# A fused layer stack: the last tiles and the last chunk of each stack issued in an order of their own

## What is computed

```python
x = x + 0.5 * _L0_ffn_ref(_layernorm(x, axis=-1), ...)   # stack 1: six layers
x = x + _L0_attn_ref(_layernorm(x, axis=-1), ...)        # a Mamba block
x = x + 0.5 * _L0_ffn_ref(_layernorm(x, axis=-1), ...)   # stack 2: the same six layers
...
for i in range(DEPTH):                                   # DEPTH = 6
    x = attn_layer(shift_tokens(x), Wqkv[i], q_scale[i], k_scale[i], Wo[i]) + x
    x = ffn_layer(shift_tokens(x), ln_g[i], ln_b[i], W1[i], b1[i], W2[i], b2[i]) + x
```

## Time and profile before

| | us |
|---|---|
| median of three runs | 3400.14 |
| lowest, highest | 3398.57, 3403.94 |
| the profiled execution | 3398.57 |
| its span, from the first to the last instruction | 3396.5 |
| stack 1 up to its last write of X | 1554.9 |
| TensorE busy | 3189.6 (94%) |
| VectorE, ScalarE, GpSimd busy | 2794.0, 2514.8, 2434.8 |

### The profile page before, as it was taken

One profiled execution on the slowest core, in us unless ns is written; L12 is line 12 of the kernel. 1 busy time (PEld: TensorE's weight loads), 2 busy tenths in 40 slices (PEclk: granted clock), 3 DMA queues, 4 the chain that ended last, 5 costly groups with the idle time before them and its releaser, 6 DMA issues.

```text
span 3396.5 us, 120279 instructions
## 1 busy us (share of the span) xinstructions
PE 3189.6 (94%) x51528; PEld 2517.5 (74%) x51528; DVE 2794.0 (82%) x3179; ACT 2514.8 (74%) x3154; POOL 2434.8 (72%) x1225
## 2 busy tenths in 40 slices
PE   7999999999999999986787999999999999999997
PEld 5888887887888888773223788878788888788775
DVE  6888888888888888865997888888888888888884
ACT  5777777777777777766775677777777777777765
POOL 6777776777777777640998777768768768678662
PEclk9999999999999999998999999999999999999999
DMA  3333233333233333221000322323323323333222
GB/s 117 88 76 88 66 88 83 77 77 91 72 83 86 77 77 76 65 64 40 8 1 1 87 72 70 94 66 88 90 70 82 91 64 89 83 77 83 68 63 55
DMA packets 142010, 245.21 MB, mean 72 GB/s; under 512 B 32365, under 2 KB 34350, under 8 KB 141358
## 3 DMA queue, kind: packets, MB, share of 16 engines
q1 hardware_dynamic: 141486, 237.51, 27.5%
HBM read 35.01 MB, written 1.05 MB: 11 GB/s over the span
## 4 chain that ended last, share of the span: by engine, by line
PE 75%; DVE 8%; issue 7%; POOL 5%; ACT 4%; DMA 0%; DVEq 0%; SPq 0%; POOLq 0%; ACTq 0%
PE PS L254 14%; PE PS L380 11%; PE PS L198 8%; PE PS L402 7%; PE PS L200 7%; PE PS L199 7%; PE PS L315 6%; PE PS L507 4%; ACT ARENA L740 2%; PE PS L441 2%; PE PS L442 2%; PE PS L443 2%; POOL ARENA L1429 2%; PE PS L420 1%; DVE ARENA L1266 1%
## 5 line engine op out<-in xcount | busy, mean ns | idle before, releaser
L1346 POOL TENSOR_TENSOR ARENA<-ARENA,RN 128x1024 f32<-128x1024 f32 x192 | 365.6, 1904 | 450.1 <-ACT RN L730 450.1
L254 PE MATMUL PS<-C,ARENA 128*128 128x128 f32 x4608 | 614.2, 276 | 35.8 <-ACT ARENA L740 15.9
L1338 POOL TENSOR_TENSOR ARENA<-ARENA 128x1024 f32<-128x1024 f32 x192 | 468.2, 2439 | 239.6 <-DVE ARENA L1050 238.8
L254 PEld LDWEIGHTS PS<-C,ARENA 128*128 128x128 f32 x4608 | 512.7, 141 | 114.2 <-issue 72.7
L198 PE MATMUL PS<-WL,XH 128*128 128x512 f32 x1152 | 489.0, 425 | 18.3 <-DVE ARENA L1050 7.2
L793 ACT ACTIVATE ARENA<-PS 64x1024 f32<-64x1024 f32 x384 | 391.0, 1018 | 108.2 <-PE PS L254 104.9
L1332 POOL TENSOR_TENSOR ARENA<-ARENA 128x1024 f32<-128x1024 f32 x192 | 457.6, 2383 | 4.1 <-DVE ARENA L1035 4.1
L200 PE MATMUL PS<-WH,XH 128*128 128x512 f32 x1152 | 455.4, 395 | 0.0
L199 PE MATMUL PS<-WH,XL 128*128 128x512 f32 x1152 | 453.1, 393 | 0.0
L380 PE MATMUL PS<-ARENA 128*64 128x64 f32 x12288 | 403.9, 224 | 48.3 <-DVE ARENA L1088 26.1
L380 PEld LDWEIGHTS PS<-ARENA 128*64 128x64 f32 x12288 | 379.1, 139 | 83.1 <-issue 82.5
(11 more groups left out here) (143 smaller groups left out, 6461.6 us busy)
## 6 DMA issues: line engine op xcount, KB each, us to landing
ARENA<-ARENA SPq DMA_DIRECT2D x1152, 128.0 KB
ARENA<-ARENA SPq DMA_DIRECT2D x768, 64.0 KB
ARENA<-in_wqkv SPq DMA_DIRECT2D x36, 512.0 KB, 4.9
ARENA<-in_wo SPq DMA_DIRECT2D x12, 512.0 KB, 4.1
ARENA<-in_w SPq DMA_DIRECT2D x12, 341.0 KB, 4.0
ARENA<-in_w SPq DMA_DIRECT2D x12, 192.0 KB, 4.3
X<-in_xT SPq DMA_DIRECT2D x4, 256.0 KB, 5.8
out<-X SPq DMA_DIRECT2D x1, 1024.0 KB, 3.9
```

What stands on the lines that cost most here:

```text
L254: last = nc.tensor.transpose(PS[:, slot, 128 * j:128 * j + 128], src[:, 128 * j:128 * j + 128], ident)
L1338: nc.gpsimd.tensor_tensor(KN[n % 2], KN[n % 2], T2, ALU.add).then_inc(k_add, 1)
```

## The change

- **An order of its own for the end.** The loops end earlier (TensorE after step 114, VectorE and ScalarE after 113, GpSimd after 112), and what is left is written out. On TensorE all scores of tile 95 stand ahead of the FFN up-projection of chunk 22, in slot 0; the FFN up-projection of chunk 22 stands behind the transposes of P of tile 94, and other stages get other slots or single banks too.
- **Units.** The last chunk is run as two units of 256 columns (`UNITS = 25`; unit 22 is chunk 22, units 23 and 24 are the halves of chunk 23), with buffers for their square, inverse root and normalised value that were free by then (`SXT`, `RST`, `XCT`). The first half is centred ahead of the output projection of tile 94.
- **X in two parts.** In the last layer X took `0.5 * A` after the FFN (L1154, L1156), where `A = y + b2 + B`. Now `half_input` adds `0.5 * B` right behind `ffn_normalise`, and `half_output` adds `y + b2` from PSUM to X in place of the two writes of A. For that the last layer's W2 and b2 are halved once: W2 in each stack by one VectorE operation (128x384) right behind `w1_low` of that layer, b2 once.
- **The store** of `out` is three transfers: columns 0 to 1535 when unit 22 is done, then each half of the last chunk. What follows a stack waits for `f_done` of unit 24 in place of `half_done`.

```diff
-STEPS = N + 25
...
+UNITS = N // 4 + 1
...
+        SXT, RST, XCT = SQ[:, 0:512], SQ[:, 512:1024], T2[:, 0:512]
+
+        def unit(u):
+            if u < UNITS - 2:
+                return 512 * (u % 4), 512, slice(0, 512)
+            o = 256 * (u - UNITS + 2)
+            return 1536 + o, 256, slice(o, o + 256)
...
+            def finish_tiles():
+                def tile(sem, n):
+                    pe.wait_ge(sem, n0 + n + 1)
+
+                def units(sem, u):
+                    pe.wait_ge(sem, c0 + u + 1)
+
+                u = UNITS - 3
+                scores_high(94)
+                tile(k_nrm, 95)
+                tile(k_rot, 95)
+                transposes(0, KN[1], kT_done)
+                tile(oT_ev, 92)
+                tile(res_done, 91)
+                units(f_ln, u)
+                out_products(92, 2)
+                tile(q_nrm, 95)
+                tile(PT_ev, 93)
+                transposes(2, QN[1], qT_done)
+                tile(sub_done, 94)
+                pe.wait_ge(v2_in[1], 160 * ((n0 + 93) // 2 + 1))
+                value_products(93)
+                tile(qT_ev, 95)
+                tile(kT_ev, 95)
+                tile(car_ev, 95)
+                score_masks(95, 0)
+                score_tiles(95, range(8), 0).then_inc(S_done, 1)
+                project(95, 2, 2, v_done)
+                tile(oT_ev, 93)
+                tile(res_done, 92)
+                out_products(93, 2)
+                tile(p_nrm, 94)
+                transposes(3, P, PT_done)
+                units(f_lo, u)
+                tile(sub_done, 95)
+                up_products(u, 1, 0)
+                tile(res_done, 93)
+                units(f_xm, u)
+                up_products(u, 2, 2)
+                tile(v_ev, 95)
+                up_products(u, 0, 4)
+                tile(PT_ev, 94)
+                pe.wait_ge(v2_in[0], 160 * ((n0 + 94) // 2 + 1))
+                value_products(94)
+                tile(p_nrm, 95)
+                units(f_h[1], u)
+                transposes(0, P, PT_done)
+                for j in range(3):
+                    units(f_h[j], u)
+                down_products(u, 3)
+                centre_product(u + 1, 4)
+                tile(oT_ev, 94)
+                out_products(94, 2)
+                tile(PT_ev, 95)
+                pe.wait_ge(v2_in[1], 160 * ((n0 + 95) // 2 + 1))
+                value_products(95)
+                units(f_sq, u + 1)
+                variance_product(u + 1, 5)
+                tile(oT_ev, 95)
+                tile(res_done, 94)
+                out_products(95, 2)
+                units(f_lo, u + 1)
+                up_products(u + 1, 0, 0)
+                up_products(u + 1, 1, 1)
+                units(f_done, u)
+                up_products(u + 1, 2, 3)
+                tile(res_done, 95)
+                units(f_xm, u + 1)
+                centre_product(u + 2, 4)
+                units(f_sq, u + 2)
+                units(f_ln, u + 1)
+                variance_product(u + 2, 5)
+                units(f_lo, u + 2)
+                up_products(u + 2, 0, 6)
+                up_products(u + 2, 1, 7)
+                up_products(u + 2, 2, 2)
+                for j in range(3):
+                    units(f_h[j], u + 1)
+                units(f_ln, u + 2)
+                down_products(u + 1, 5)
+                for j in range(3):
+                    units(f_h[j], u + 2)
+                units(f_xm, u + 2)
+                down_products(u + 2, 4)
...
-            for s in range(STEPS):
+            for s in range(115):
...
+            k_evacuate(95, 0)
+            exponentials(94)
+            q_evacuate(95)
+            high_part(u)
+            o_evacuate(93)
+            v_evacuate(95)
+            exponentials(95)
+            p_evacuate(94, 3)
+            gelu(u, 1, 0)
+            gelu(u, 2, 2)
+            gelu(u, 0, 4)
+            o_evacuate(94)
+            p_evacuate(95, 0)
+            tables(act)
+            square(u + 1, 4)
+            o_evacuate(95)
+            inverse_root(u + 1, 5)
+            high_part(u + 1)
+            square(u + 2, 4)
+            inverse_root(u + 2, 5)
+            high_part(u + 2)
+            gelu(u + 1, 0, 0)
+            gelu(u + 1, 1, 1)
+            gelu(u + 1, 2, 3)
+            gelu(u + 2, 0, 6)
+            gelu(u + 2, 1, 7)
+            gelu(u + 2, 2, 2)
+            if r == 0:
+                tables(act)
...
+            def half_input(u):
+                q0, w, x = unit(u)
+                k = u - 4 * (NL - 1)
+                dve.wait_ge(res_done, n0 + min(4 * u + 4, N - 2 if u == UNITS - 2 else N))
+                nc.vector.scalar_tensor_tensor(X[0:64, q0:q0 + w], B[0:64, q0:q0 + w], 0.5, X[0:64, q0:q0 + w],
+                                               ALU.mult, ALU.add)
+                nc.vector.scalar_tensor_tensor(X[64:128, q0:q0 + w], B[64:128, q0 + 1:q0 + w + 1], 0.5,
+                                               X[64:128, q0:q0 + w], ALU.mult, ALU.add).then_inc(x_half, 1)
...
             def ffn_normalise(x):
+                if 0 <= x < N and x % 4 == 3:
+                    normalise(x // 4, 3)
+                    if x // NT == NL - 1:
+                        half_input(x // 4)
...
+            def half_output(u, bank):
+                q0, w, x = unit(u)
+                b2 = LP[:, (NL - 1) * NP + P_B2:(NL - 1) * NP + P_B2 + 1]
+                dve.wait_ge(f_y, c0 + u + 1)
+                dve.wait_ge(b2_half, 1)
+                dve.wait_ge(x_half, 5 * r + u - 4 * (NL - 1) + 1)
+                nc.vector.scalar_tensor_tensor(X[0:64, q0:q0 + w], PSB[0:64, bank, 0:w], b2[0:64, :],
+                                               X[0:64, q0:q0 + w], ALU.add, ALU.add)
+                nc.vector.scalar_tensor_tensor(X[64:128, q0:q0 + w], PSB[64:128, bank, 0:w], b2[64:128, :],
+                                               X[64:128, q0:q0 + w], ALU.add, ALU.add).then_inc(f_done, 1)
...
             def ffn_residual(x):
+                if l == NL - 1:
+                    half_output(c, 3)
+                    return
...
-                if l == NL - 1:
-                    dve.wait_ge(f_done, c0 + c + 1)
-                    nc.vector.scalar_tensor_tensor(X[0:64, q0:q0 + 512], A[0:64, q0:q0 + 512], 0.5,
-                                                   X[0:64, q0:q0 + 512], ALU.mult, ALU.add)
-                    nc.vector.scalar_tensor_tensor(X[64:128, q0:q0 + 512], A[64:128, q0 + 1:q0 + 513], 0.5,
-                                                   X[64:128, q0:q0 + 512], ALU.mult, ALU.add).then_inc(half_done, 1)
-                elif c % 4 == 3:
+                if c % 4 == 3:
                     w1_low(l + 1)
+                    if l + 1 == NL - 1:
+                        dve.wait_ge(wo_in[1], 32 * (3 * r + 3))
+                        nc.vector.tensor_scalar(W2[1], W2[1], 0.5, None, ALU.mult, ALU.bypass).then_inc(w2_half, 1)
...
+            k_rotate2(95)
+            k_sums(95)
+            floor_sums(95)
+            residual(91)
+            row_sums(93)
+            row_max(94)
+            subtract_max(94)
+            normalise(u, 3)
+            residual(92)
+            row_sums(94)
+            row_max(95, 0)
+            subtract_max(95, 0)
+            residual(93)
+            half_input(u)
+            row_sums(95)
+            gate(u, 1, 0)
+            gate(u, 2, 2)
+            gate(u, 0, 4)
+            half_input(u + 1)
+            half_output(u, 3)
+            residual(94)
+            normalise(u + 1, 4)
+            residual(95)
+            half_input(u + 2)
+            normalise(u + 2, 4)
+            gate(u + 1, 0, 0)
+            gate(u + 1, 1, 1)
+            gate(u + 1, 2, 3)
+            half_output(u + 1, 5)
+            gate(u + 2, 0, 6)
+            gate(u + 2, 1, 7)
+            gate(u + 2, 2, 2)
+            half_output(u + 2, 4)
...
+            k_add_halves(95)
+            p_normalise(93)
+            k_normalise(95)
+            q_normalise(95)
+            low_part(UNITS - 3)
+            p_normalise(94)
+            p_normalise(95)
+            low_part(UNITS - 2)
+            low_part(UNITS - 1)
...
-            sp.wait_ge(half_done, 8)
-            sp.dma_start(out, X[:, :]).then_inc(out_put, 16)
-            sp.wait_ge(out_put, 16)
+            for u, a, b in ((UNITS - 3, 0, 1536), (UNITS - 2, 1536, 1792), (UNITS - 1, 1792, 2048)):
+                sp.wait_ge(f_done, UNITS + u + 1)
+                sp.dma_start(out[:, a:b], X[:, a:b]).then_inc(out_put, 16)
+            sp.wait_ge(out_put, 48)
```

302 lines of the change are left out of this document (172 added, 130 removed).

## The result

The changed kernel took 3384.32 us (median of 4 runs, 3381.31 to 3385.01), the kernel before, beside it, 3400.18 (4 runs, 3398.57 to 3403.94): ratio 0.995, 95% interval 0.9933 to 0.9967. That is 15.9 us faster where 28 were forecast. The changed kernel's profiled execution took 3384.22, and its span is 14.15 us shorter than that of the earlier trace rows.

What follows compares the result with a forecast made beforehand. TensorE, busy 94% of the time, was taken as the bound, so only its waits or clock matter. Terms -21.3 - 15.9 + 5.6 + 5.5 - 2.0 = -28.1 gave 3372 us against the median; range 3362 to 3385.

Steps and rivals of the forecast that it cites:

- the four places: End of each stack, residual step losing X writes, normalise step gaining them, halving of W2; the store a small fifth.
- A: Stack ends gain half: 256-column units cost nearly what 512 did, TensorE at 1.2 GHz there; 3381 us, chance 20%.
- rival B: Normalise step: GpSimd wins the race each time and TensorE's clock falls; 3384 us, chance 17%.
- the signs for being right the first: Stack end: 47 to 49 us from the start of tile 94's upper scores to the last write of X.
- Part 1: End of each stack: new order shortens it by 11.0 us in stack 2, 10.3 in stack 1; -21.3 us.
- I take 0.6: 12.9 us: Stack end, second half's centring to last write: 0.6 of the 21.4 us at 512 columns.
- 1.8 us per stack: Stack end: charge for TensorE's low clock after two idle gaps, before the second half's up-projection and down-projection.
- Rival C: A wait written out in finish_tiles holds TensorE for a stage, end chain as long as before; 3393 us, 5%.
- Parts 2 and 3: Chunks 20 and 21: X writes leave the residual step, -15.9 us, and come to the normalise step, +5.6 us.
- Part 4: Halving W2 once per stack delays the row maxima, 2.0 us each plus 1.5 for a clock fall; +5.5 us.
- Part 5: Final store: only 128 KB left for the end, 1.9 us instead of 3.9; -2.0 us, bounds 0 and -3.

Runs made afterwards that it cites:

- x8: Changed kernel plus, in each stack's end, ten unread 256-column products in TensorE's two waits; 3378.81 us, ratio 0.9922.
- x1: Changed kernel with residual(91) first in VectorE's tail and floor_sums(95) behind the row sums; 3380.34 us, ratio 0.9935.
- x2: Changed kernel with half_input of chunks 20 and 21 moved one step later, behind the gates; 3377.68 us, ratio 0.9931.
- x3: Changed kernel with half_input of chunks 20 and 21 right ahead of half_output in the residual step; 3378.75 us, ratio 0.9931.
- x4: Changed kernel with half_input of chunks 20 and 21 behind the FFN output write, ahead of row_max; 3390.54 us, ratio 0.9966.
- x0: The changed kernel run again without edits; 3382.93 us, ratio 0.9946 to the kernel before.
- x6: Changed kernel with the last chunk as one 512-column unit instead of two of 256, output in two transfers; 3382.86 us, ratio 0.9945.
- x5: Changed kernel with the halving of W2 moved from VectorE to ScalarE behind its own weight split; 3374.49 us, ratio 0.9917.

## Why the prediction was right in direction and too large

The sign and the four places were right, and 14 of 28 us were missing. The table above says where; they are separate misses, not one. The time lay 0.7 us inside the range, and outside the forecast's own 3365 to 3378: the range reached it only because it was stretched to rivals A and B, and neither of them is what happened. That it held is luck in part. Of the signs for being right the first was missed (50.4 and 50.6 us for 47 to 49), the others held.

- **Part 1, the end (-17.7 for -21.3).** The layout of the dense part held: P of tile 95 at 19.2 us behind the start (forecast 19.9), out 95 at 28.5 (29.0), second centring at 33.7 (34.0). The step that failed is the size of the last term, "I take 0.6: 12.9 us" with "1.8 us per stack" for the clock: 14.7 forecast, 16.6 measured. x8 splits it: 14.1 at full clock (a factor of 0.66) and 2.5 for the clock. So waits between stages of half the columns, and the clock behind them, were each priced too low.
- **Part 1 again, a wait that was not in it (+3.8).** The layout began at the upper scores of tile 94 and so left out what the new order did ahead of them: `residual(91)` behind three other operations (x1). Rival C named this kind of wait, but on TensorE's written-out list and as one that would eat the whole gain; it came from VectorE's list, and cost 1.9 per stack. The order of VectorE's tail was in the diff; the question "what is queued ahead of an operation that TensorE waits for" was not asked of it.
- **Parts 2 and 3, X (-10.7 for -10.3).** Right in both: by x2 as the base, the writes cost 262.64 - 246.15 = 16.5 us before (forecast 15.9) and 5.8 after (forecast 5.6). Only the wording was wrong: x3 and x4 show that the cost sits behind the wait for the down-projection and ahead of the row maxima, not in the step as such, and that some 1.4 us of lateness of the row maxima there is free.
- **Part 4, W2 (+7.3 for +5.5).** The 2.05 us was right; the clock term was too small. Nine traces have this operation on VectorE with `w1_low` ahead of it (the changed kernel, x0 to x4, x6 to x8), two stacks each. From values 79 to 83 they take 65.1 us in the four stretches without a low-clock window (2.0 above the kernel before), 66.0 to 66.2 in the six with one of 3.4 us, 67.5 to 67.6 in the eight with one of 6.8 us. So a fall cost 1.0 or 2.4, and it came in 14 of 18 and not in one of two. The forecast had 1.5 for both stacks; the changed kernel's trace has 3.4. x5 shows the larger point, that the operation and `w1_low` ahead of it together cost 4.6 and 6.0, clock falls included.
- **Part 5, the store (-1.65 for -2.0).** Right.
- **The rest (+4.8).** 1.65 us at the ramp (the stretch up to values 0), 2.46 between the stacks, 0.7 in the steady part, all put at 0. The ramp was 65.3 to 69.3 in kernels that don't differ there: 68.4 to 69.3 in the seven whose low-clock window near 55 us lasts 6.8 us, 65.3 to 67.3 in the six where it lasts 3.4. The halving of b2, which the forecast put at 0, lies in the ramp too, and no run isolates it. Between the stacks it is not mere variation: 346.8 to 348.6 in the twelve kernels whose last chunk is in two units, 345.6 before and 344.0 in x6, whose last chunk is whole. The low-clock windows lie elsewhere too, at 129 to 137 and 242 to 250 us behind the last write of X in the changed kernel, at 183 to 189 before and in x6. Why splitting the last chunk should lengthen the stage behind it stays open.

The time of rival B (3384) is the measured one, but its mechanism did not happen: VectorE won the race in the normalise step each time. Nor was it A as priced, whose ends gain 12 us in all; they gained 17.7, although the two things that A names, half units that cost more than half and the low clock, are what made the ends too long. Two of the prediction's sums don't come out of their own terms. For A, a factor of 0.85 and 3 us for the clock give 4.3 + 3.2 - 3 = 4.5 per end, 9 in all and 3384, where it says 6.0, 12 and 3381 (that needs 3 us for both ends together). And a factor of 0.5 without a clock charge gives 3364 for the lower end of the range, not 3362.

## What to carry to other kernels

Lay out a new order from the first instruction that moved on any engine, not from where the gain is expected, and ask of each operation that TensorE waits for what now stands ahead of it in its own queue. Where an operation of VectorE and one of GpSimd hold each other up, as `w1_low` and L1562 did in x5, a start 0.2 us earlier or later can be worth 2 us to one of them, so an operation without urgency belongs in VectorE's wait for TensorE, ahead of that wait, or on ScalarE. Where a sparse end is left, splitting the work further gave about 1.5 us per stack here, with the clock low behind the gaps; keeping TensorE busy there gave about 2.6. The whole chunk with TensorE kept busy was not tried.

## What the runs showed of the hardware

- A 128x32 operation with one SBUF input (L1238, 0.12 us alone) took 1.31 us, in both stacks, and ended as GpSimd's L1568 did; the same kind of operation on 128x384 took 2.05 and 2.50 beside GpSimd, and ScalarE did that work in 0.51.
- The last down-projection (three products, six records) took 2.82 us with 512 columns at full clock (x6), and with 256 columns 2.90 at the low clock (changed kernel) and 1.54 at the full one (x8): in the end of this kernel half the columns at half the clock is no gain.
- Ten products whose results nobody reads, put into two waits of TensorE, kept the granted clock at 1.00 over 17 us, where it was 0.76, and made the ends 2.5 and 3.4 us shorter than the changed kernel's, 2.6 against the mean of nine kernels with the same end.
- One fall of the clock behind the halving of W2 cost 1.0 us where its low window was 3.4 us long and 2.4 where it was 6.8, alike within 0.2 us over 18 stretches of nine traces.
